# Stage 2's layers in a Perceiver kernel: three rounded products for each, in place of Strassen's sums in fp32

## What is computed

```python
h = silu(_tlin(x, w1_w, w1_s)) * _tlin(x, w2_w, w2_s)      # 256 -> 1024
h = gelu(_tlin(h, h1_w, h1_s))                             # 1024 -> 1024
h = gelu(_tlin(h, h2_w, h2_s))                             # 1024 -> 1024
return _tlin(h, w3_w, w3_s)                                # 1024 -> 256
# _tlin(x, w, s) = einsum('bsi,oi->bso', x, w) * s; x = layernorm of the stream, the result is added to it
```

## Time and profile before

| what | us |
|---|---|
| median of three runs | 1490.05 |
| lowest, highest run | 1487.29, 1491.04 |
| span of the profiled execution, first to last instruction | 1484.2 |
| TensorE busy | 1414.7 (95%) |
| VectorE, ScalarE, GpSimd busy | 1000.6, 775.5, 331.7 |
| mean granted clock of TensorE | 0.988 |

### The profile page before, as it was taken

How to read it: one execution, slowest core, us unless ns; L and a number is a source line. 1 busy time by engine, 2 the same in 40 slices (tenths; PEclk the granted TensorE clock), 3 DMA queues, 4 the chain that set the end, 5 groups by cost and what they waited for, 6 DMA issues and landing times.

```text
span 1484.2 us, 26603 instructions
## 1 busy us (share of the span) xinstructions
PE 1414.7 (95%) x10631; PEld 994.1 (67%) x10641; DVE 1000.6 (67%) x1735; ACT 775.5 (52%) x1445; POOL 331.7 (22%) x439
## 2 busy tenths in 40 slices
PE   7899999999999999999999989999999999999998
PEld 5787666887898766898656745555555554655697
DVE  5776645454687575787367578889999982566533
ACT  5574342112565355565355447777777776315222
POOL 3784330001643123733203041010000000100000
PEclk9999999999999999999999999999999999999999
DMA  9314132221122320221215376455667503210140
GB/s 370 137 57 183 65 113 85 87 87 56 65 86 88 149 84 30 74 80 56 105 52 172 78 183 98 76 87 86 166 95 144 113 5 143 126 58 2 58 170 15
DMA packets 43009, 147.76 MB, mean 100 GB/s; under 512 B 6380, under 2 KB 21996, under 8 KB 34028
## 3 DMA queue, kind: packets, MB, share of 16 engines
q1 hardware_dynamic: 42888, 146.07, 34.2%
HBM read 123.49 MB, written 22.56 MB: 98 GB/s over the span
## 4 chain that ended last, share of the span: by engine, by line
PE 81%; DVE 9%; ACT 4%; POOL 3%; issue 2%; DMA 0%; SPq 0%; POOLq 0%; ACTq 0%; DVEq 0%
PE PS L163 51%; PE PS L2484 8%; PE PS L2396 7%; PE PS L2381 5%; PE PS L635 2%; DVE SM L2500 2%; PE PS L1966 1%; POOL CNr L933 1%; PE PS L1987 1%; PE PS L2475 1%; PE PS L3070 1%; PE PS L1994 1%; PE PS L2975 1%; DVE ARr L1795 0%; DVE AR L1105 0%
## 5 line engine op out<-in xcount | busy, mean ns | idle before, releaser
L2500 DVE TENSOR_REDUCE SM<-PS 128x1 f32<-128x1024 f32 x256 | 301.6, 1218 | 32.8 <-PE PS L2381 31.5
L163 PE MATMUL PS<-ARr 128*128 128x256 f32 (+1 forms) x800 | 220.7, 325 | 0.8 <-POOL CNr L933 0.7
L163 PE MATMUL PS<-CNr,ARr 128*128 128x256 f32 (+1 forms) x728 | 152.5, 305 | 14.3 <-DVE ARr L802 9.9
L2396 PE MATMUL PS<-AR 49*128 49x256 bf16 (+1 forms) x1216 | 162.9, 271 | 1.4 <-DVE AR L2521 0.7
L163 PEld LDWEIGHTS PS<-ARr 128*128 128x128 f32 x800 | 139.5, 190 | 12.2 <-issue 1.1
L163 PEld LDWEIGHTS PS<-CNr,ARr 128*128 128x128 f32 x728 | 114.2, 199 | 20.1 <-DVE ARr L802 13.3
L2396 PE MATMUL PS<-AR,CT 49*128 49x256 bf16 (+1 forms) x832 | 124.2, 271 | 0.0
L163 PE MATMUL PS<-ARr,HTr 128*128 128x512 f32 x384 | 122.5, 400 | 0.5 <-issue 0.5
L863 ACT CAST ARr<-PS 128x512 fp32r<-128x512 f32 x96 | 56.3, 586 | 117.5 <-PE PS L635 117.5
L163 PE MATMUL PS<-AR 128*128 128x256 f32 (+3 forms) x504 | 109.4, 371 | 1.4 <-DVE AR L721 0.8
L2573 ACT ACTIVATE AR<-PS 128x512 f32<-128x512 f32 x172 | 93.5, 601 | 23.2 <-PE PS L2396 23.2
(11 more groups left out here) (418 smaller groups left out, 2790.6 us busy)
## 6 DMA issues: line engine op xcount, KB each, us to landing
CN<-ctx_n SPq DMA_DIRECT2D x24, 1024.0 KB, 5.5
AR<-k_parts SPq DMA_DIRECT2D x114, 128.0 KB
k_parts<-CN SPq DMA_DIRECT2D x32, 384.0 KB, 3.3
CT<-pack SPq DMA_DIRECT2D x6, 2048.0 KB, 7.7
AR<-pack SPq DMA_DIRECT2D x20, 512.0 KB, 4.6
CT<-k_parts SPq DMA_DIRECT2D x78, 128.0 KB
CT<-ctx_t SPq DMA_DIRECT2D x8, 1024.0 KB, 19.5
v_ones<-CN SPq DMA_DIRECT2D x28, 288.0 KB, 3.3
```

What stands on the lines that cost most here:

```text
L163: last = te.matmul(o, l, r, start=first and k == 0, stop=final and k == n - 1, skip_group_check=True)
L2396: return te.matmul(PS[:, b, z * 256:z * 256 + 256], keys[rows, c * 128:c * 128 + 128], QQ9[rows, pr, rest, cols], start=not rest, stop=boo ...
L2500: ve.tensor_reduce(MX9[:, p % 2, e, g % 8 // 4, g % 4:g % 4 + 1], PS[:, b:b + 2, :].rearrange("p a b -> p (a b)"), AX, ALU.max).then_inc(* ...
```

## The change

Stage 2 multiplies in three float32r products throughout, as stages 0 and 3 do, and the Strassen sums are gone.
- w1 and w2 are loaded into CN at the end of stage 0 (two loads of 1 MB), and GpSimd splits them in stage 1: `weights_pool_1`, eight times a cast and a subtraction of 512 columns, between its eight additions and the job of t1b.
- HT is split by ScalarE (heads) and VectorE (rests). In up each bank gets six matmuls. The head of the product h is a ScalarE copy, its rest a VectorE subtraction.
- Each layer is 8 banks of 24 matmuls with 512 columns. ScalarE runs the Gelu twice, once into float32r (HH2) and once into fp32 (HF2), and VectorE subtracts. The layer weights come in 512 KB pieces n = 0 to 15 through a ring of three buffers; ScalarE makes the head (`head_of_layer`), VectorE the rest (`rest_of_layer`).
- w3 is loaded earlier, in two halves, and split by GpSimd (`weights_pool_2`) behind the jobs of b2 and t2; each of the four banks gets 24 matmuls with 256 columns.
- The context of stage 3 is loaded behind the last bank of the second layer, ("hp_ps", 1, 7). Stage 3's tiles in AR move.

The core of the diff:

```diff
@@ -964,7 +964,7 @@
-                    sp.wait_ge(("mix", s, 2 * q + 1, 1) if b else ("mix", s - 3, 9 + 2 * q, 1))
+                    sp.wait_ge(("mix", s, 2 * q + 1, 1) if b else ("hp_ps", 1, 7) if s == 3 else ("mix", s - 3, 9 + 2 * q, 1))
...
@@ -987,7 +987,10 @@
             sp.wait_ge(("s_ps", 0, 15, 1))
...
-            load_context(sp, 3, 0)
+            for q in range(2):
+                at = SPAN["s2"][0] + 2048 * q
+                sp.wait_ge(("mix", 0, 9 + 2 * q, 1))
+                se.dma_start(CNf[:, 2048 * q:2048 * q + 2048], pack[:, at:at + 2048]).then_inc(*sp.lands(f"w12_{q}", "w12", q))
...
@@ -1171,6 +1174,7 @@
             for i in range(4):
                 pl.wait_ge(("xy", 1, i), ("c2g", 1))
                 ge.tensor_tensor(Y1[:, i, :], Y1[:, i, :], W1["c2b"], ALU.add).then_inc(*pl.inc("row", "xyb", 1, i))
+            weights_pool_1(pl)
             jobs_pool(pl, "t1b")
             pl.end(1)
@@ -1185,203 +1189,112 @@
         sm_begin()
         s2_rs = sm(4)
...
+        HF2 = [view(a, 0, 8, 512) for a in (AR, CNf, AR)]
+        HR2 = [view(a, 0, 8, 512) for a in (ARr, CNrf, ARr)]
+        HH2 = [view(a, 4096, 8, 512) for a in (ARr, CNrf, ARr)]
+        HWF = [AR[:, 8192 + 2048 * k:9216 + 2048 * k] for k in range(3)]
+        HWR = [ARr[:, 8192 + 2048 * k:9216 + 2048 * k] for k in range(3)]
+        HWH = [ARr[:, 9216 + 2048 * k:10240 + 2048 * k] for k in range(3)]
...
+        def turn_head_act(ac, s, dst):
+            for i in range(4):
+                ac.wait_ge(("ht_ps", s, i))
+                ac.e.copy(dst[:, :, tok(i)], bank("ht", s, i)[:, 0:256].rearrange("p (k t) -> p k t", k=2)).then_inc(
+                    *ac.inc("turn", "hth", s, i))
+        def turn_rest_dve(dv, s, head, dst):
+            for i in range(4):
+                dv.wait_ge(("hth", s, i))
+                dv.e.tensor_tensor(dst[:, :, tok(i)], bank("ht", s, i)[:, 0:256].rearrange("p (k t) -> p k t", k=2),
+                                   head[:, :, tok(i)].bitcast(F32), ALU.subtract).then_inc(*dv.inc("turn", "ht", s, i))
+        def thirds(lh, lr, rh, rr):
+            return [(lh, rh), (lh, rr), (lr, rh)]
         def pe_2(pe):
             te = pe.e
             begin_pe(pe, 2)
             turn_all(pe, 2, "ht", H, "h")
             jobs_pe(pe, "t2")
...
+            for m in range(8):
+                for k, kind in enumerate("gu"):
+                    b, before = PB.take((kind, 2, m), ("g", 2, m) if kind == "g" else ("h0", 2, m))
+                    pe.wait_ge(*before, *ht_all(2), ("w12r", 7))
+                    mm(te, PS[:, b, :], [p for kt in range(2) for p in thirds(
+                        W12H[k][:, kt, tok(m)], W12R[k][:, kt, tok(m)], HTH2[:, kt, :], HTR2[:, kt, :])]).then_inc(
+                        *pe.inc("proj", kind + "_ps", 2, m))
...
+                for m in range(8):
+                    n = 8 * l + m
+                    wh, wr = mat(HWH[n % 3], 8), mat(HWR[n % 3], 8)
+                    b, before = PB.take(("hp", l, m), ("hh", l + 1, m))
+                    pe.wait_ge(*before, ("hwr", n))
+                    for k in range(8):
+                        pe.wait_ge(("hr", l, k))
+                        z = mm(te, PS[:, b, :], thirds(wh[:, k, :], wr[:, k, :], HH2[l][:, k, :], HR2[l][:, k, :]),
+                               k == 0, k == 7)
+                    z.then_inc(*pe.inc("proj", "hp_ps", l, m))
...
+                for k in range(8):
+                    c = slice(k % 4 * 256, k % 4 * 256 + 256)
+                    pe.wait_ge(("hr", 2, k))
+                    z = mm(te, PS[:, b, 0:256], thirds(HH2[2][:, k, tok(i)], HR2[2][:, k, tok(i)], W3H[k // 4][:, c],
+                                                       W3R[k // 4][:, c]), k == 0, k == 7)
+                z.then_inc(*pe.inc("proj", "y_ps", 2, i))
...
+            def rest_of_hidden(l, m):
+                dv.wait_ge(("hh", l, m))
+                ve.tensor_tensor(HR2[l][:, m, :], HF2[l][:, m, :], HH2[l][:, m, :].bitcast(F32), ALU.subtract).then_inc(
+                    *dv.inc("rest", "hr", l, m))
+            def rest_of_layer(n):
+                dv.wait_ge(("hwh", n))
+                ve.tensor_tensor(HWR[n % 3], HWF[n % 3], HWH[n % 3].bitcast(F32), ALU.subtract).then_inc(
+                    *dv.inc("rest", "hwr", n))
+            for m in range(8):
                 dv.wait_ge(("g", 2, m), ("u_ps", 2, m), ("w2s", 2))
...
+                if m in (2, 4, 6):
+                    rest_of_layer(m // 2 - 1)
+                if m:
+                    rest_of_hidden(0, m - 1)
+            rest_of_hidden(0, 7)
+            for n in range(16):
+                rest_of_hidden(n // 8 + 1, n % 8)
+                if 3 <= n + 2 < 16:
+                    rest_of_layer(n + 2)
...
+            def head_of_layer(n):
+                ac.wait_ge(("hw", n), ("hp_ps", (n - 3) // 8, (n - 3) % 8) if n > 2 else None)
+                ae.copy(HWH[n % 3], HWF[n % 3]).then_inc(*ac.inc("head", "hwh", n))
+            def head_of_product(m):
+                ac.wait_ge(("h0", 2, m))
+                ae.copy(HH2[0][:, m, :], HF2[0][:, m, :]).then_inc(*ac.inc("gelu", "hh", 0, m))
+            for m in range(8):
                 ac.wait_ge(("g_ps", 2, m), ("w2s", 2))
...
+                if m in (1, 3, 5):
+                    head_of_layer(m // 2)
+                if m:
+                    head_of_product(m - 1)
+            head_of_product(7)
...
+            for n in range(16):
+                l, m = n // 8, n % 8
+                scale = W2["h1s" if l == 0 else "h2s"][:, m:m + 1]
+                ac.wait_ge(("hp_ps", l, m))
+                ae.activation(HH2[l + 1][:, m, :], bank("hp", l, m), ACT.Gelu, scale=scale)
+                ae.activation(HF2[l + 1][:, m, :], bank("hp", l, m), ACT.Gelu, scale=scale).then_inc(
+                    *ac.inc("gelu", "hh", l + 1, m))
+                if 3 <= n + 2 < 16:
+                    head_of_layer(n + 2)
             end_act(ac, 2)
+        def weights_pool_1(pl):
+            pl.wait_ge(("mix", 0, 15, 1))
+            for k in range(8):
+                raw, c = CNf[:, 512 * k:512 * k + 512], slice(512 * k, 512 * k + 512)
+                head = CNrf[:, 4096 + 512 * k:4608 + 512 * k]
+                pl.wait_ge(("w12", k // 4))
+                pl.e.tensor_copy(head, raw).then_inc(*pl.inc("split", "w12h", k))
+                pl.wait_ge(("w12h", k))
+                pl.e.tensor_tensor(CNrf[:, c], raw, head.bitcast(F32), ALU.subtract).then_inc(
+                    *pl.inc("split", "w12r", k))
+        def weights_pool_2(pl):
+            for j in range(2):
+                for k in range(2):
+                    c = slice(512 * k, 512 * k + 512)
+                    pl.wait_ge(("w3", 2, j), ("u_ps", 2, 7))
+                    pl.e.tensor_copy(W3H[j][:, c], W3F[j][:, c]).then_inc(*pl.inc("split", "w3h", j, k))
+                    pl.wait_ge(("w3h", j, k))
...
         def pool_2(pl):
             jobs_pool(pl, "b2", *ht_all(2))
             jobs_pool(pl, "t2")
+            weights_pool_2(pl)
             pl.end(2)
...
+            se.dma_start(SC2, pack[:, s0 + 6144:s0 + SPAN["s2"][1]]).then_inc(*sp.lands("w2s", "w2s", 2))
+            def layer(n):
+                at = SPAN["s2h"][0] + n * 1024
+                if n > 2:
+                    sp.wait_ge(("hp_ps", (n - 3) // 8, (n - 3) % 8))
+                se.dma_start(HWF[n % 3], pack[:, at:at + 1024]).then_inc(*sp.lands(f"hw{n % 3}", "hw", n))
+            for n in range(3):
+                layer(n)
+            sp.wait_ge(("ht_ps", 2, 3))
+            se.dma_start(W3F[0], pack[:, s0 + 4096:s0 + 5120]).then_inc(*sp.lands("w23_0", "w3", 2, 0))
...
+            for n in range(3, 16):
+                if n == 4:
                     jobs_sp(sp, "s2")
...
+                layer(n)
+            sp.wait_ge(("hp_ps", 1, 5))
             se.dma_start(*w3_load).then_inc(*sp.lands("w3", "w", 3))
```

More of the change, by code:

```diff
@@ L1197, in perceiver @@
-        RS1, RS6, RS7 = view(Hf, 0, 4, 256), view(AR, 12288, 4, 256), view(AR, 13312, 4, 256)
-        UP2 = (0, 4, 1, 5, 2, 6, 3, 7)
-        ST2 = banks.ring(*[(k,) for k in range(8)])
-        def half(l, j):
-            return slice(256 * (j ^ l), 256 * (j ^ l) + 256)
-        def quarters(l, a, k0=0, k1=4):
-            return [a[:, 4 * i + k0:4 * i + k1, half(l, j)] for i in range(2) for j in range(2)]
-        def places_2(l, m):
-            return [(hB2, hA2)[l][:, m + 4 * i, half(l, j)] for i in range(2) for j in range(2)]
@@ L1212, in rows_2 @@
-        def rows_2(l, part, ks=range(4)):
-            if l == 0:
-                return [("h0", 2, k + 4 * (part > 20)) for k in ks]
-            return [("h1", {11: 12, 12: 11, 21: 22, 22: 21}[part], k) for k in ks]
+        SC2, W2, at2 = sm(288), {}, 0
+        for name, cols in PACK["s2"][3:]:
+            W2[name] = SC2[:, at2:at2 + cols]
+            at2 += cols
+        W12R = [view(CNrf, 2048 * k, 2, 1024) for k in range(2)]
```

(15 more changed lines are left out.)

189 lines of the change are left out of this document (19 added, 170 removed).

## The result

The changed kernel takes 1480.76 us (median of 4 runs, 1476.63 to 1482.91), the kernel before 1488.67 us beside it (4 runs): a ratio of 0.9938 with an interval of 0.9918 to 0.9958, faster by 7.9 us. In a second set with more runs it was 1481.78 against 1488.19 us, 0.9959 [0.9943, 0.9976], faster by 6.4 us. The forecast was 1483.4 us.

What follows compares the result with a forecast made beforehand. TensorE was taken to bound stage 2. Matmuls at -15.3 us plus 8.7 us of delay from the end of stage 1 gave -6.6 us, so 1483.4 us; range 1475 to 1491, the forecast case's own 1479 to 1488.

Steps and rivals of the forecast that it cites:

- up: Stage 2's first products, with w1 and w2: 16 banks of six rounded matmuls take 22.6 us in place of 27.5.
- layers, waits on rests with them: Stage 2's two layers: matmuls take 88.5 us in place of 97.5, plus 0.4 us for waits on rests.
- w3: Stage 2's last product: eight groups of twelve matmuls at 1.50 us each take 12.0 us in place of 13.8.
- matmuls together: Up, layers, w3 and added waits in stage 2: 123.5 us against 138.8, a gain of 15.3 us.
- GpSimd's eight pairs: End of stage 1: eight casts and subtractions splitting w1 and w2 take 15.2 us, plus 0.7 us held up by VectorE.
- TensorE idle: Ahead of stage 2: GpSimd's late job delays VectorE's norm, leaving TensorE idle from 214.79 to 221.4, some 6.6 us.
- half clock: Behind the wait at stage 2's entry: the granted clock falls to 0.50 and costs 2.35 us, between nothing and 2.4.
- delay of up: Stage 2's entry: up starts 8.6 us later than at 217.88; with 0.1 us for rounding, 8.7 us.
- rival with 0.216 us: 512-column matmuls take 0.216 us, 480 of them giving 6.3 us: 1477.1 us; chance 0.13 (faster matmuls).
- rival of no cheaper products: Stage 2's matmuls take 0.25 us in place of 0.229, a weight load standing out: 10 us more, 1493.5; chance 0.06.
- rival of a longer tail: GpSimd's splits in stage 1: heads cost 1.16 us, not 0.61, plus 1.2 us more held-up instructions: 1489.0 us; chance 0.16.
- dry ring: Layer loads n = 3 to 15 land too late for the three buffers: 17.2 us lost at 11.2 us landing, 1500.6; chance 0.08.

Runs made afterwards that it cites:

- two buffers: The changed kernel with two layer-weight buffers in place of three and stage 3's weights loaded behind bank (1, 7) in place of (1, 5): 1480.62 us, single run.
- keep-warm: The changed kernel with 26 unused matmuls on TensorE between the jobs of b2 and the wait of stage 2: 1482.4 us (7 runs).
- two products: The changed kernel with the third product (weights' rest by rows' head) left out in both layers: 1452.88 us (4 runs).
- early splits: The changed kernel with GpSimd's splits of w1 and w2 behind the job of t1 instead of ahead of the job of t1b: 1476.94 us (6 runs).
- third trace of the kernel before: The kernel before, unchanged, run once more for its trace alone: 1494.32 us in a single run.
- w3 in fp32: The changed kernel with the w3 product again in fp32, without splits of w3 and rests of the last hidden rows: 1480.54 us, single run.
- 40 matmuls: The changed kernel with 40 unused one-column matmuls in TensorE's idle time ahead of stage 2: 1480.85 us (5 runs).

## Why the prediction held, and where it was off

| term | predicted | measured | from |
|---|---|---|---|
| up | 22.6 | 22.2 | TensorE's timeline |
| layers, waits on rests with them | 88.9 | 88.7 | same |
| w3 | 12.0 | 11.0 | same |
| matmuls together | -15.3 | -17.2 | 123.4 against 140.6, the value job with them |
| GpSimd's eight pairs | 15.9 | 16.2 | 196.98 to 213.19 |
| TensorE idle | 6.6 | 6.4 | 211.99 to 218.39 |
| half clock | 2.35 | 0.8 to 0.95 (2.3 in the two buffers trace) | 3.85 against 3.09 us; keep-warm run |
| delay of up | 8.7 | 7.2 | 10.25 against 3.09 |
| net | -6.6 | -10.0 local | 133.66 against 143.66 |

**The matmuls.** The rows of stage 0 carried over: matmuls of 512 columns start 0.227 us apart (0.229 predicted), and the two products run shows that nothing else bounds the layers but for at most 1.4 us. The rival with 0.216 us did not come. The Trainium skill (TensorE: Matmul & The Clock Gate, Back-to-back issue gap) gives 216 ns for an isolated matmul of this size; the trace has 0.227 us over a whole stage. A weight load behind each matmul did not raise the price, so the rival of no cheaper products did not come either. The term that was mis-sized is w3: I took groups of twelve from stage 0, 1.50 us each. In w3 96 matmuls of 256 columns take 11.03 us, 0.115 us each, so a group takes 1.38; that the other 0.12 us belong to the change from one kind of work to another in stage 0 is my reading, and not shown. The value job behind up also took 0.2 us less to the next start (1.53 in place of 1.73 us), and the -17.2 holds that, which the -15.3 didn't count.

**The end of stage 1.** The mechanism came as described: GpSimd's job late, VectorE's L297 behind it, TensorE idle. The early splits show it by taking it away, with the same work. For instructions held up by VectorE I had taken 0.7 us; four pairs of 0.2 us are 0.8. GpSimd's cast into float32r took the 0.61 us of its cast into bf16, so the rival of a longer tail did not come.

**The half clock** was mis-sized: 2.35 us predicted, 0.8 to 0.95 measured. The clock did fall to 0.50. The loss that I carried over came from a stretch with 4.7 us of matmuls at 0.50. In the change the clock was back at 1.00 by 222.0 us, before up began at 222.24. The eight transposes took 1.74 us from first to last (218.39 to 220.13) where they take 1.06 in the third trace of the kernel before; the job behind them, to up's start, 2.11 in place of 2.03, and up's first matmul, to the next, 0.63 in place of 0.34 in the keep-warm run. Where the clock stayed low for longer, in the two buffers trace (0.50 to about 226.2 us, where up began at 224.77), the loss was 2.3 us, nearly what I had put. So it was not the amount of work behind the wait that made it small, since up follows at once in both, but how soon the clock rose. By the same count, to up's third matmul, 0.7 to 1.0 us were lost in the five other traces with this wait (the change twice, two products, w3 in fp32, 40 matmuls). Why it rose later in the one, the rows don't tell.

**From the stretch to the whole.** The local gain is 10.0 us, the medians show 7.9 and 6.4 (interval 3.6 to 8.5). The two mis-sized terms (-1.9 of matmuls and value job, -1.5 of clock) are as large as the difference of forecast and local result. Outside the stretch the prediction put nothing, and there the medians have 2.1 and 3.6 us of loss. So the total came near by luck: the local gain was put too low by 3.4 us, and a loss elsewhere of nearly that size was not in the sum at all. The traces don't say where it lies. Outside the local stretch the ten traces of changed kernels have 3.4 us more on average than the first one of before, with -4.2 to +9.1 us among them, and the three of before 3.3 (0, 1.5 and 8.3); with so few and such a spread, a loss of 2 to 5 us can't be seen in them. Its cause stays open.

**The rest.** Loads landed in 3.4 us (4.6 before), and stage 3's mixes showed no wait for their context, so both were rightly put at nothing. The dry ring got 0.08 and a price from a wrong cycle; the two buffers run gives the right one, which makes it rarer to be slower: by it the ring would cost more than the local gain of 10 us only above L = 10.9 us, and loads landed in 3.4.

## What to carry to other kernels

When work is added to an engine that is mostly idle, look at what stands behind it in that engine's queue: 16 us of splits on a GpSimd that is busy 24% held the whole core for 6 us from one place in its queue and 0.1 to 0.8 us from another. Judge each part of a change by the part's own balance; here the faster product of up was a loss, while those of the layers and w3 were gains, and the sum hid it. Compare the stretch that was changed first, and take at least two more traces of the unchanged kernel before explaining a difference anywhere else. Then hold the stretch against the medians: where they show less than it, as here, something outside it has changed too, though no single trace may show where.
